# A graph network on one core: gathers of the two edge passes without a landing wait, and their loads cut into sixteen-partition DMAs

## The reference

```
x = x + gcn3(h)        # three graph convolutions
x = x + gcn2(h)        # two graph convolutions
x = x + network(h)     # two "propagate" passes over all edges, with dense layers between
x = x + attention(h)   # two heads, softmax over the edges of each node
```

```
z     = silu([h_i, h_j, a] @ We + be)
msg   = (a @ Wl) * z
out_i = mean of msg over the edges of i, + h_i
```

## Time and profile before

| | us |
|---|---|
| median of two runs (16301.63, 16309.38) | 16305.5 |
| the profiled execution, its own time | 16222.93 |
| its span | 16221.2 |

### The profile page before, as it was taken

One profiled execution on the slowest core, in us unless ns is written; L12 is line 12 of the kernel. 1 busy time (PEld: TensorE's weight loads), 2 busy tenths in 40 slices (PEclk: granted clock), 3 DMA queues, 4 the chain that ended last, 5 costly groups with the idle time before them and its releaser, 6 DMA issues.

```text
span 16221.2 us, 180153 instructions
## 1 busy us (share of the span) xinstructions
PE 9592.5 (59%) x40895; PEld 6450.1 (40%) x40896; DVE 7215.4 (44%) x18628; ACT 3844.3 (24%) x8556; POOL 9525.9 (59%) x8465
## 2 busy tenths in 40 slices
PE   0466657766478878845555556655555545555555
PEld 0111122221133333335555554555555545555554
DVE  8876657777000000013333332333333357777776
ACT  0344444442011111112222222222222212222221
POOL 0378878888645434426666664566666645555553
PEclk9999999999688778865555555555555555555555
DMA  9922222222599989992222223222222344444444
GB/s 385 358 15 19 19 15 20 20 20 18 168 342 370 343 306 357 359 113 86 84 86 84 85 84 50 75 84 86 84 86 85 80 95 139 141 141 140 140 139 96
DMA packets 1483063, 2197.01 MB, mean 135 GB/s; under 512 B 882955, under 2 KB 926027, under 8 KB 1454669
## 3 DMA queue, kind: packets, MB, share of 16 engines
q1 hardware_dynamic: 907628, 1490.52, 28.2%
q0 software_dynamic: 453120, 343.50, 12.7%
q10 hardware_dynamic: 121698, 356.43, 6.0%
HBM read 1771.19 MB, written 419.98 MB: 135 GB/s over the span
## 4 chain that ended last, share of the span: by engine, by line
POOL 40%; DMA 22%; issue 21%; PE 8%; DVE 4%; another core or an unknown queue 3%; ACT 1%; POOLq 0%; SPq 0%; DVEq 0%; ACTq 0%
POOL gat L645 18%; POOL adj L613 12%; POOL arena L645 8%; DMA arena<-adj 8%; DMA gat<-q_table,ring_i 6%; DMA arena<-h_table,ring_i 5%; PE bank L1029 5%; DMA adj<-put_n,put_at 2%; POOL rec_src L599 1%; DVE arena L1356 1%; PE same L1161 1%; PE same L1000 1%; DVE arena L1358 1%; PE same L980 0%
## 5 line engine op out<-in xcount | busy, mean ns | idle before, releaser
L645 POOL DMA_INDIRECT gat<-q_table,ring_i x3456 | 3626.6, 1049 | 2405.7 <-DMA gat<-q_table,ring_i 1025.0
L613 POOL DMA_INDIRECT adj<-put_n,put_at x1632 | 2559.9, 1569 | 1265.3 <-DVE put_at L1440 638.1
L1183 PE MATMUL bank<-onehot_t,onehot 128*128 128x64 f32 x6912 | 1585.5, 424 | 2574.9 <-DVE acc L1578 1880.5
L1183 PEld LDWEIGHTS bank<-onehot_t,onehot 128*128 128x128 f32 x6912 | 1506.7, 330 | 2653.8 <-DVE acc L1578 1938.5
L599 POOL DMA_INDIRECT rec_src<-pay,ring_i x1632 | 1606.4, 984 | 1566.9 <-ACTq L743 1093.2
L645 POOL DMA_INDIRECT arena<-h_table,ring_i x1728 | 1729.4, 1001 | 1346.2 <-DMA arena<-h_table,ring_i 760.8
L1088 PE MATMUL same<-onehot 32*128 32x512 f16 x3264 | 1678.6, 615 | 620.0 <-DVE onehot L1411 389.3
L1029 PE MATMUL bank<-arena,hs 128*64 128x512 f32 x5880 | 1596.0, 707 | 508.2 <-DMA arena<-adj 506.9
L1419 DVE TENSOR_SCALAR_CACHE_REDUCE onehot<-same 128x128 bf16<-128x128 f32 (+3 forms) x1632 | 1233.0, 756 | 843.2 <-PE same L1090 675.9
L1173 PE MATMUL bank<-hs,arena 128*128 x6912 | 1564.0, 421 | 29.3 <-ACT arena L867 29.3
L1173 PEld LDWEIGHTS bank<-hs,arena 128*128 128x128 f32 x6912 | 1525.9, 333 | 29.8 <-issue 29.8
(11 more groups left out here) (277 smaller groups left out, 13003.2 us busy)
## 6 DMA issues: line engine op xcount, KB each, us to landing
arena<-adj SPq DMA_DIRECT2D x300, 2560.0 KB
arena<-rec_src SPq DMA_DIRECT2D x432, 552.0 KB
adj<-hs ACTq DMA_DIRECT2D x25, 6656.0 KB, 46.3
rec_src<-pay ACTq DMA_DIRECT2D x1, 119232.0 KB, 332.0
arena<-lo_row SPq DMA_DIRECT2D x432, 256.0 KB
hs<-b_row SPq DMA_DIRECT2D x108, 1024.0 KB
acc<-b_row SPq DMA_DIRECT2D x108, 1024.0 KB
gat<-q_table,ring_i POOLq DMA_INDIRECT x3456
```

What stands on the lines that cost most here:

```text
L613: nc.gpsimd.indirect_dma_start(counts, bass.IndirectOffsetOnAxis(put_at[:, b // 3 % 4, c:c + 1], 0), put_n[:, b // 3 % 4, c:c + 1], None, ...
L645: nc.gpsimd.indirect_dma_start(rows[n][:, u, :], None, table, bass.IndirectOffsetOnAxis(ring_i[:, n, u:u + 1], 0)).then_inc(landed[n], 16)
L1183: last = mm(bank[6 + n % 2][:, u // 2 * D:(u // 2 + 1) * D], onehot[:, n % 2, u, :], msg[n % 2][:, u, :], start=u % 2 == 0, stop=u % 2 == 1)
```

## The change

POOL's gathers of the two passes no longer wait for the landing of the previous group's; the wait for the index stays. In the attention layer nothing changes: the parameter is renamed there, and the call passes the same values as before. SP's two loads of a group become sixteen: eight of 16 partitions for the record, then eight of 16 partitions for the place row. The bytes are the same. The waits on their semaphores go by 16 x 8 in place of 16 for a group.

```
+SPLIT = 8
+SLICE = P // SPLIT
...
             def load_edges(k, i, n):
-                sp.dma_start(pay4[n], rec[:, bass.ds(i * (4 * U) + n * U, U), :]).then_inc(l_pay[n], 16)
-                sp.dma_start(lo_bc[n], lo_rows[bass.ds(i * 4 + n, 1), :].to_broadcast([P, U * P])).then_inc(l_lo[n], 16)
+                for q in range(SPLIT):
+                    ps = slice(q * SLICE, (q + 1) * SLICE)
+                    sp.dma_start(pay4[n][ps], rec[ps, bass.ds(i * (4 * U) + n * U, U), :]).then_inc(l_pay[n], 16)
+                for q in range(SPLIT):
+                    ps = slice(q * SLICE, (q + 1) * SLICE)
+                    sp.dma_start(lo_bc[n][ps], lo_rows[bass.ds(i * 4 + n, 1), :].to_broadcast([SLICE, U * P])).then_inc(l_lo[n], 16)
...
-            def gathers(table, rows, landed, i, n, before, first):
-
-                if not first:
+            def gathers(table, rows, landed, i, n, before, free):
+
+                if not free:
                     hold(pool, landed[(n - 1) % len(landed)], i * (16 * U) + before)
...
-            def node_rows(k, i, n, first=False):
+            def node_rows(k, i, n):
                 hold(pool, l_idx, i * 4 + (k * NG + n + 1))
-                gathers(q_table[k], gat4, l_gat, i, n, (k * (NG // 4) + (n > 0)) * 16 * U, first)
+                gathers(q_table[k], gat4, l_gat, i, n, 0, True)
...
-                    act.wait_ge(l_lo[n], i * 16 + (k * (NG // 4) * 16 + 16))
+                    act.wait_ge(l_lo[n], i * (16 * SPLIT) + (k * (NG // 4) + 1) * 16 * SPLIT)
...
-                    dve.wait_ge(l_pay[n], i * 16 + (k * (NG // 4) * 16 + 16))
+                    dve.wait_ge(l_pay[n], i * (16 * SPLIT) + (k * (NG // 4) + 1) * 16 * SPLIT)
```

More of the change, by code:

```diff
@@ L655, in _ @@
                 for n in range(4):
-                    node_rows(k, 0, n, first=k == 0 and n == 0)
+                    node_rows(k, 0, n)
                 with pool.Fori(1, NG // 4) as i:
```

## The result

| | us |
|---|---|
| before, median | 16305.5 |
| changed, median (15286.65, 15310.28) | 15298.5 |
| predicted (range) | 15745 (15470 to 16120) |

The changed kernel takes 0.938 of the time before, 95% interval 0.9353 to 0.9408. It is 1007 us faster, where 561 were forecast. The direction, the bound and the worth of the landing wait were right.

A forecast was written before the change was run, and what follows sets the result against it. The prediction took POOL's gathers, with the landing wait on their path, as the bound. 801 us for the wait less 240 for harder DVE collisions gave 561 off 16305.5, about 15745 us, range 15470 to 16120.

The forecast's parts named there:

- the bound: In the passes POOL, with its gathers, bounds the kernel at 12.87 us a group, and stays the bound at 11.5.
- the worth of the landing wait: Before each steady group POOL's gap falls from 2.24 to 0.30 us, 1.94 a group over 413 groups: 801 us.
- the late place row: Place load behind the record's slices comes about 10.5 us after the message; ACT's work is covered by 2 us, cost nothing.
- Padding gains almost nothing: At the ends of passes gathers queue, so no gain was counted for some 16 groups; 896 us in all if they gained.
- DVE's blocks hit POOL harder: In the passes, time gathers are held by DVE rises from 0.82 to 1.4 us a group, a loss of 240 us.
- It doesn't slip between back-to-back instructions: A gather held by DVE waits until the whole block ends; based on one attention-layer gather of 3.31 us.
- the forecast distance: The block of lines 1558 and 1568 starts 1.46 us after a group's last gather ends, holding a gather for 1.08.
- rival 2: DVE's blocks lie kindly to POOL's gathers, under 0.9 us held a group, and padding gains too: 15235 to 15500; chance 0.07.
- the collisions (1): DVE's blocks fall at their worst on POOL's gathers, 1.9 up to 2.6 us a group: 15950 to 16240; chance 0.10.
- the SP bound (3): SP's sixteen issues, 0.80 us apart, become the bound at a period of 13.0 us: about 16360; chance 0.09.
- Slices that run one behind another (4): SP's sixteen slices don't overlap, 2.02 us each, 32 us a group: about 24700; chance 0.02.
- change its name (5): POOL's wait only turns from landing to index or a limit of transfers under way, no difference: 16305; chance 0.04.

The follow-up runs named there:

- the first experiment: The changed kernel with SP's record and place loads whole again (one DMA of 128 partitions each), POOL still without the landing wait; 15303.6 us, ratio 0.9406.
- the met wait: The changed kernel with a landing wait of POOL put back, for the group two before and not the previous one; 15295.4 us, ratio 0.9353.

## Why the prediction was wrong

**Right.** The bound (POOL) and the worth of the wait. A met wait is hidden, now shown by the wait on the group two before. `l_idx` is met in the steady groups. SP's sixteen issues take 7.55 us for 7.5 forecast, the late place row costs nothing, and nothing else becomes the bound. Padding gains almost nothing: from the first gather of the first pass to the first of the second is 3017.5 us before (10228.22 - 7210.73) and 2521.5 after (9651.49 - 7129.98), 496 less, and 207 groups at 2.35 are 486 of it. The landing wait at the end of a pass became a wait for the index.

**The step that failed** is "DVE's blocks hit POOL harder", and in it the sentence "It doesn't slip between back-to-back instructions". It does. The block of lines 1564 and 1574 came near the forecast distance in 75 of 190 groups. The price there was not 1.08 but at most 0.5, to the end of one instruction (1.43 less 0.95 at 8013.07). In the others the block came a few tenths later and all but missed the points. From 7300 to 9300 us this block cost 0.16 a group, and that of line 1556 cost 0.34, for 0.43 forecast. The whole term was 1.4 a group and measured 0.52: 0.88 x 413 = 363 us. The stop that vanished adds 0.09 x 432 = 39. With the 561 that is 963 us. The runs gave 1007, then 965 in the series of the first experiment (16268 - 15304) and 1056 in that of the met wait (16351 - 15295). The changed kernel and those two lie within 9 us, so it is the kernel before that moved: its period was 12.93 in its second profile, for 12.87.

**How it came about.** The slip was denied on one row, the gather of 3.31 us beside a block of four. It is among the longest gathers of the trace. Taken as a whole, the same trace says the opposite: in its attention layer, of 79 gathers held in the first instruction of that block, 68 were released at its end (0.69) and 11 at the block's (2.5). Nine more, whose needy point came in the second or third instruction, were held to the block's end too. And in the ten other profiles no gather of the attention layer is over 1.5 us. What set those twenty apart stays open, but it wasn't chance. All of them lie in the fifth of every eight groups, at one place of the layer's loop. There 11 of 15 gathers held in the first instruction waited for the whole block, and at the other places none of 64 did. Why that place, and why in this profile alone, was not tried. The prediction's own rows of the passes agreed with both readings, because both held gathers there had come in the second instruction of their block.

The bounds had held the truth for this term (from nothing to 2.6), but the kind case was given 0.07 and the range ended above it. That case, rival 2, has the measured time (15235 to 15500) and the held time (under 0.9), but not the reason: with whole loads the block lay in its bad place in 141 of 189 groups and the term was still 0.60, and padding hardly gained. Of the other rivals, the collisions (1) and the SP bound (3) did not come true at eight slices. Slices that run one behind another (4) are excluded by the period of 10.52 us. The fit of 2.0 us that the prediction quotes stands in the Trainium skill, page "DMA: Bandwidth & Descriptors", section "Anatomy of one DMA — SWDGE (gpsimd) path", for DMAs issued from POOL, and these are SP's. The slices of 69 and 32 KB alone cost no time (ratio 0.9982). The wait did not change its name (5) outside the padding groups.

## What to carry to other kernels

Before a wait is priced, look at what the waiting engine collides with, and read a collision from the distribution of all such cases, not from the longest one. A wait for a transfer's landing is free if it asks for one group further back than the transfers take, and then it needs no removal. Where POOL issues many gathers, vector instructions with both inputs in SBUF should be short, or have one input in PSUM; the PSUM input was worth 0.8% here. And when one wait is taken away, follow the chain again: in the attention layer it went to a row's way through HBM.

## What the runs showed of the hardware

- A gather needs something that DVE holds about 0.13 us after its start, and gets it when the running instruction ends: at 0.69 for 512 columns, at 1.22 for 1024. It slips in between two instructions without a gap, except in twenty cases of one profile. An input in PSUM frees it (held time 0.5 to 0.1 a group). If DVE's instruction began at most 0.17 us before that point, the gather was not held (80 of 80 at line 1564). The Trainium skill, page "SBUF — State Buffer", section "SBUF: two separate sides", calls it a shared port pair, an exclusive lock for the whole instruction, and names a vector instruction with two SBUF inputs among those that take it, but only against a GpSimd instruction that reads SBUF. The traces agree in the unit, the instruction and not the block. These gathers take their row indices from `ring_i` in SBUF; that this read is what waits was not tried.
- DMAs of SP cost it about the same whatever their size: 0.28 us busy for 8 partitions, 0.32 to 0.37 for 16 and 0.33 for 128, with 0.09 to 0.19 between two.
- Gathers of padding groups, whose 128 rows are all the same row, land late: the last eight groups of a pass took 16.8 us each with the landing wait, against 12.87 for the others. That the same row is the reason was not tried.
- The kernel before had medians that differed between series by 83 us (16268 and 16351), and each series ran on its own chip, so small effects are read only within one series.
